# Gated cross-attention and gated MLP on one core: V and A of the decay-weighted output product as pairs of f16 parts in place of fp32r

## The reference, cut to what matters

```
xh, kh   = layernorm(x), context                     # 4 heads of 128 columns
Q,K,V    = xh @ Wh, kh @ Wh, kh @ Wh                 # per head
masked   = (Q @ K^T / sqrt(128)) * decay             # [b, h, s, t]
A        = maximum(abs(masked.sum(axis=0)), 1.0)     # summed over the 64 tiles
O        = A @ V                                     # per head, one A for all tiles
Y        = (O - mean) / sqrt(var + 0.001) * gamma + beta
x        = x + tanh(g0) * (relu(xh @ wg) * Y @ wo)
x        = x + tanh(g1) * (silu(ln(x) @ gate^T * gs) * (ln(x) @ up^T * us)) @ down^T * ds
```

## Time and profile before

| | |
|---|---|
| time, median of 3 | 1442.77 us |
| profiled execution, span | 1447.4 us, granted clock 0.998 |
| TensorE matmul busy | 1420.4 us, 98% |
| VectorE, ScalarE, GpSimd busy | 1043.3, 726.3, 735.3 us |
| attention loop | to about 323 us |
| first `o(0)` | 328.65 us |

### The profile page before, as it was taken

The page is one execution under the profiler, slowest core; times in us unless marked ns, Lnnn a source line. Parts: engine busy times, 40 slices in busy tenths (PEclk is TensorE's granted clock), DMA queues, the critical chain, the costliest instruction groups (busy, mean ns, idle before and its releaser), DMA issues.

```text
span 1447.4 us, 20320 instructions
## 1 busy us (share of the span) xinstructions
PE 1420.4 (98%) x7097; PEld 728.3 (50%) x7135; DVE 1043.3 (72%) x1562; ACT 726.3 (50%) x1145; POOL 735.3 (51%) x734
## 2 busy tenths in 40 slices
PE   8999999999999999999999999999999999999998
PEld 4666666665445544455444444444444444444443
DVE  7788998878477676766776677564867768768762
ACT  5566565554555635455463545534344444443442
POOL 5656769863564445444553554434137237137235
PEclk9999999999999999999999999999999999999999
DMA  8999898973878796987888897886383473572432
GB/s 275 344 336 306 292 317 318 343 251 130 276 204 263 227 276 206 260 276 210 248 274 237 264 243 222 247 252 164 112 228 115 124 224 122 139 218 98 139 109 89
DMA packets 372920, 324.96 MB, mean 225 GB/s; under 512 B 259280, under 2 KB 285264, under 8 KB 372816
## 3 DMA queue, kind: packets, MB, share of 16 engines
q1 hardware_dynamic: 355248, 291.63, 66.2%
q10 hardware_dynamic: 17568, 31.99, 6.2%
HBM read 209.14 MB, written 114.43 MB: 224 GB/s over the span
## 4 chain that ended last, share of the span: by engine, by line
PE 74%; DVE 10%; DMA 6%; SPq 3%; issue 3%; ACT 2%; POOL 2%; ACTq 0%; DVEq 0%; POOLq 0%
PE ps L2067 24%; PE po L2067 8%; PE pyb L1930 7%; PE ps L2074 7%; PE ptb L2074 5%; PE pyb L2074 5%; PE ps L1988 5%; PE po L1930 3%; PE pyb L2058 3%; PE ptb L2058 3%; DMA wy_scratch<-misc 2%; SPq L510 2%; DVE reg L1129 1%; PE ptb L2062 1%; PE pyb L2062 1%
## 5 line engine op out<-in xcount | busy, mean ns | idle before, releaser
L2067 PE MATMUL ps<-x2t,gate 128*128 128x512 f16 x704 | 166.6, 379 | 1.2 <-DVE tmp L1436 1.1
L1930 PE MATMUL pyb<-xnt,wgs 128*128 128x512 f16 x708 | 166.3, 380 | 1.4 <-DVE wgs L1153 1.3
L2067 PE MATMUL ps<-op,wbuf 128*128 128x512 f16 x704 | 166.3, 379 | 0.5 <-issue 0.5
L2067 PE MATMUL ps<-x2t,up 128*128 128x512 f16 x704 | 166.3, 379 | 0.0
L1800 POOL TENSOR_TENSOR p5b<-p5b,p1b 128x512 f32<-128x512 f32 x44 | 55.7, 1265 | 209.1 <-ACT p5b L860 209.1
L1816 POOL TENSOR_TENSOR hid<-tmp,hid 128x512 f16<-128x512 f32 x88 | 104.6, 1190 | 105.9 <-ACT hid L836 105.9
L2074 PE MATMUL ps<-down_first,hid 128*128 128x512 bf16 x683 | 152.4, 379 | 2.1 <-POOL hid L1816 0.8
L1811 POOL TENSOR_TENSOR hsp<-hall,hsp 128x640 f16<-128x640 f32 (+2 forms) x72 | 123.6, 1731 | 37.1 <-ACT hsp L887 37.1
L2067 PE MATMUL po<-op,wbuf 128*128 128x512 f16 x528 | 129.0, 379 | 0.6 <-DVE u2b L1383 0.6
L1436 DVE SCALAR_TENSOR_TENSOR tmp<-ps,colsb,tmp 128x512 f32<-128x512 f32 x88 | 65.4, 744 | 68.2 <-PE ps L2067 62.3
L1988 PE MATMUL ps<-reg 128*128 128x256 f32 x768 | 109.7, 294 | 4.3 <-DVE reg L1129 3.8
(11 more groups left out here) (218 smaller groups left out, 2764.2 us busy)
## 6 DMA issues: line engine op xcount, KB each, us to landing
wbuf<-ws_scratch SPq DMA_DIRECT2D x44, 896.0 KB, 5.0
xr<-in_x SPq DMA_DIRECT2D x62, 512.0 KB, 6.3
raw<-in_ctx_t SPq DMA_DIRECT2D x32, 512.0 KB, 5.6
v_scratch<-tmp ACTq DMA_DIRECT2D x64, 256.0 KB, 6.0
raw<-v_scratch SPq DMA_DIRECT2D x32, 512.0 KB, 6.6
x_scratch<-xr SPq DMA_DIRECT2D x32, 512.0 KB, 4.8
xr<-x_scratch SPq DMA_DIRECT2D x32, 512.0 KB, 5.9
raw<-w_scratch SPq DMA_DIRECT2D x31, 512.0 KB, 6.0
```

What stands on the lines that cost most here:

```text
L1930: last = e.matmul(dst, lhs[a], rhs[b], start=(k == 0 and i == 0), stop=(k == n - 1 and i == 2))
L2067: last = e.matmul(dst, upper(wt), act[i], start=start, stop=stop and exact, skip_group_check=True)
```

## The change

V and A become pairs of f16 parts. f16 has a small range, so each is first multiplied by one number for the whole tensor.

- *V.* ScalarE squares the whole context with an accumulated sum (`ct_square`, two 128x1024 passes per group, written where `ct_hi` writes afterwards; `ct_hi` waits for it). VectorE adds the 32 sums (`ac`), TensorE adds them over partitions (`ct_bound`), VectorE multiplies by a factor from Wh (`am`), GpSimd makes `vk` of it (power -1/2). `v_hi` is an ACTIVATE with scale `vk`, `v_lo` a SCALAR_TENSOR_TENSOR.
- *A.* VectorE takes the row maximum, TensorE turns it (`a_bound`), VectorE reduces it, makes a power of two of it (`ak`) and writes the two parts. The 0.001 of the normalisation becomes a value `eg` from both factors.
- *Order.* `v_hi(0)` comes behind two V evictions and waits for `vk`. GpSimd waits for `am` in front of `weights_residue(6)`. The loads of group 1's context wait for the squares of group 0. Two more quarters of W tile `LATE + 2` run before `o(0)`, and the later quarters move up by one or two places. Two semaphores are merged into others.

```diff
-        a_sb = [placed(f"a{i}", [128, 512], f32r) for i in range(2)]
+        a_parts = [over(f"a_part{i}", f"a{i}", 0, [128, 4, 128], f16) for i in range(2)]
-        vs_later = [part(52 + 4 * i, 512, b=2) for i in range(2)]
+        vs_later = [over(f"vs_later{i}", "reg", 52 + 4 * i, [128, 2, 512], f16) for i in range(2)]
@@ SP: ct_load
                 if g == 1:
+                    p.wait_ge("mass", 7)
@@ ScalarE
+            def ct_square(g, hp):
+                p.wait_ge(f"ct{hp}", 16 * (g + 1))
+                if g >= 2:
+                    p.wait_ge("v", 4 * g - 4)
+                e.activation(ct[1 if g == 0 else g % 2][0][:, 2 * hp:2 * hp + 2, :], raw[:, 2 * hp:2 * hp + 2, :], ACT.Square, scale=2.0 ** -15,
+                             accum_out=csq[:, 2 * g + hp:2 * g + hp + 1]).then_inc(s["mass"])
 ct_hi:
+                p.wait_ge("mass", 5 + 2 * g + h // 2 + 1)
 v_hi:
-                e.copy(vs_of(q)[0], raw[:, 0:2, :]).then_inc(s["vhi"])
+                p.wait_ge("cc", 2)
+                e.activation(vs_of(q)[0][:, :, :], raw[:, 0:2, :], ACT.Identity, scale=vk).then_inc(s["vhi"])
 order, group 0:
             w_store(0)
+            ct_square(0, 0)
+            ct_square(0, 1)
             w_out(1)
...
             w_out(2)
+            ct_square(1, 0)
             ct_hi(1, 0)
...
             v_out(2)
+            ct_square(1, 1)
             ct_hi(1, 2)
 order, groups from 1:
-                else:
-                    v_hi(0)
...
                 v_store(4 * g)
                 if not more:
+                    v_hi(0)
                     w_out(LATE - 1)
...
                 v_store(4 * g + 1)
+                ct_square(g + 1, 0)
                 ct_hi(g + 1, 0)
...
                 v_out(4 * g + 2)
+                ct_square(g + 1, 1)
                 w_out(4 * g + (1 if g < NG - 2 else 0))
@@ VectorE, last group
+                    p.wait_ge("mass", 5 + 2 * NG)
+                    e.tensor_reduce(ac, csq[:, :], AX.X, ALU.add).then_inc(s["cs"])
                 v_acc(4 * g)
+                    p.wait_ge("bound", 3)
+                    e.tensor_scalar(am, ptb[:, 1, 0:1], fk, 1e-30, ALU.mult, ALU.add).then_inc(s["cs"])
@@ VectorE, A
-            e.tensor_scalar(a_sb[0][:, :], xr[:, 7, :], 1.0, None, ALU.max).then_inc(s["ahi"])
-            e.scalar_tensor_tensor(a_sb[1][:, :], xr[:, 7, :], 1.0, f(a_sb[0][:, :]), ALU.max, ALU.subtract).then_inc(s["alo"])
+            p.wait_ge("cc", 2)
+            e.tensor_reduce(am, xr[:, 7, :], AX.X, ALU.max).then_inc(s["ad"])
+            e.tensor_scalar(xr[:, 7, :], xr[:, 7, :], 1.0, None, ALU.max).then_inc(s["ad"])
+            p.wait_ge("bound", 4)
+            e.tensor_reduce(ak[:, 0:1], ptb[:, 1, :], AX.X, ALU.max).then_inc(s["ahi"])
+            e.tensor_scalar(ak[:, 1:2], ak[:, 0:1], 1.0, 2.0 ** -14, ALU.max, ALU.mult).then_inc(s["ahi"])
+            e.tensor_single_scalar(ak[:, 2:3].bitcast(u32), ak[:, 1:2].bitcast(u32), 0x7F800000, ALU.bitwise_and).then_inc(s["ahi"])
+            e.reciprocal(ak[:, 3:4], ak[:, 2:3]).then_inc(s["ahi"])
+            e.tensor_scalar(a_parts[0][:, :, :], wide, ak[:, 3:4], None, ALU.mult).then_inc(s["ahi"])
+            e.scalar_tensor_tensor(a_parts[1][:, :, :], wide, ak[:, 3:4], a_parts[0][:, :, :], ALU.mult, ALU.subtract).then_inc(s["alo"])
@@ GpSimd
+            p.wait_ge("cs", 3)
+            e.tensor_scalar(vk, am, 2.0 ** 30, 1e-30, ALU.mult, ALU.add).then_inc(s["cc"])
+            e.tensor_tensor(vk, vk, nhalf[:, 0:1], ALU.pow).then_inc(s["cc"])
             weights_residue(6)
@@ TensorE
                 v(4 * g + 1, 1)
                 if not more:
+                    ct_bound()
...
-            w(LATE + 2, (0,))
+            a_bound()
+            w(LATE + 2, (0, 1, 2))
             o(0)
...
-            w(LATE + 2, (1, 2, 3))
+            w(LATE + 2, (3,))
+            w(LATE + 3, (0, 1))
             y_t(0)
-            w(LATE + 3, (0, 1))
+            w(LATE + 3, (2,))
             o(1)
-            w(LATE + 3, (2,))
+            w(LATE + 3, (3,))
             y_t(1)
-            w(LATE + 3, (3,))
+            w(LATE + 4, (0,))
             wo_mm(0, (0, 1))
-            w(LATE + 4, (0,))
             y_t(2)
```

More of the change, by code:

```diff
@@ L14 @@
 SEMAPHORES = (
-    ["xt0", "xt1", "xt2", "whr", "whr2", "wgr0", "wgr1", "wgr2", "wgr3", "cols", "rows", "dec", "wor", "dld", "outb", "lowld", "vld"]
+    ["xt0", "xt1", "xt2", "whr", "whr2", "wgr0", "wgr1", "wgr2", "wgr3", "cols", "dec", "wor", "dld", "outb", "lowld", "vld"]
     + [f"xl{i}" for i in range(4)]
@@ L26 @@
     + ["st", "mv", "xn", "tbxe", "tbwe", "tb2e", "scaledlo", "whlo", "ctlf", "zlo", "acc", "and", "xlo", "lowm"]
-    + ["ad", "ahi", "alo", "flag", "vlo", "wolo", "nm", "nr", "aff", "wm", "wylo", "wyb", "x2b", "x1", "st2", "mv2", "nm2", "xn2", "ds", "h", "hlo"]
-    + ["mass", "bound", "lim"]
+    + ["ad", "ahi", "alo", "flag", "vlo", "wolo", "nm", "nr", "aff", "wm", "wylo", "wyb", "x2b", "x1", "st2", "mv2", "nm2", "xn2", "h", "hlo"]
+    + ["mass", "bound", "lim", "cs", "cc"]
     + ["oe", "of", "gs", "top", "topd", "all", "inv", "dpk", "dmv"])
@@ L148, in gated_layer @@
         down = over("down", "xreg", 0, [128, NI, 512])
-        a_sb = [placed(f"a{i}", [128, 512], f32r) for i in range(2)]
+        for i in range(2):
+            placed(f"a{i}", [128, 512])
         xbuf = placed("xbuf", [128, 2, 512])
-        a_parts = [a[:, :].rearrange("p (h n) -> p h n", h=4) for a in a_sb]
+        a_parts = [over(f"a_part{i}", f"a{i}", 0, [128, 4, 128], f16) for i in range(2)]
         reg = placed("reg", [128, 84 * 256], f32r)
@@ L173, in gated_layer @@
         down_first = over("down_first", "reg", 33, [128, NI, 512], bf16)
-        vs_later = [part(52 + 4 * i, 512, b=2) for i in range(2)]
+        vs_later = [over(f"vs_later{i}", "reg", 52 + 4 * i, [128, 2, 512], f16) for i in range(2)]
         x2t = [over(f"x2t{i}", "reg", 68 + 8 * i, [128, 4, 512], f16) for i in range(2)]
         wos = [[over(f"wos{i}{k}", "reg", 4 + 8 * i + k, [128, 512], f16)[:, :] for k in range(4)] for i in range(2)]
-        vs_first = [part(36 + 4 * i, 512, b=2) for i in range(2)]
+        vs_first = [over(f"vs_first{i}", "reg", 36 + 4 * i, [128, 2, 512], f16) for i in range(2)]
         wyt_first = [over(f"wyt_first{i}", "reg", 32 + 2 * i, [128, 4, 128], f16) for i in range(2)]
@@ L213, in gated_layer @@
         yb = tmp[:, 3, :]
+        csq = sb("csq", [128, 2 * NG])
+        scales = sb("scales", [128, 16])
+        fk, am, ac, vk, ak, eg = [scales[:, a:b] for a, b in ((0, 1), (1, 2), (2, 3), (3, 4), (4, 8), (8, 10))]
         sums = [over(f"sums{i}", "wyt0", 12 * i, [128, 6, 4, 128]) for i in range(2)]
@@ L550, in _ @@
             e.dma_start(colsb[:, :], cols).then_inc(s["cols"], 16)
-            e.dma_start(ds[:, :], rows).then_inc(s["rows"], 16)
+            e.dma_start(ds[:, :], rows).then_inc(s["cols"], 16)
             x_load(6)
@@ L899, in silu @@
                 p.wait_ge("gm", m + 1)
-                p.wait_ge("gs", 1)
+                p.wait_ge("gs", 2)
                 if m >= 3:
@@ L1139, in limit_g @@
                 power_above(0, ptb[:, 0, 0:1].bitcast(u32), 0)
+                e.tensor_scalar(fk, ptb[:, 0, 0:1], 2.0 ** -16, 1e-30, ALU.mult, ALU.add).then_inc(s["cs"])
             def limit_wg(step):
@@ L1432, in hidden @@
                 m, n = 11 * g + j, 15 * g + j
-                p.wait_ge("gs", 2)
+                p.wait_ge("gs", 3)
                 p.wait_ge("si", m + 1)
@@ L1440, in finish @@
                 p.wait_ge("dn", t + 1)
-                p.wait_ge("ds", 1)
+                p.wait_ge("gs", 1)
                 p.wait_ge(*yb_read[0])
@@ L1507, in _ @@
                     stats(n + 4)
+                if not more:
+                    p.wait_ge("mass", 5 + 2 * NG)
+                    e.tensor_reduce(ac, csq[:, :], AX.X, ALU.add).then_inc(s["cs"])
                 v_acc(4 * g)
                 if not more:
+                    p.wait_ge("bound", 3)
+                    e.tensor_scalar(am, ptb[:, 1, 0:1], fk, 1e-30, ALU.mult, ALU.add).then_inc(s["cs"])
                     low_sums(3, 2)
@@ L1604, in _ @@
             v_lo(3)
-            p.wait_ge("rows", 16)
+            p.wait_ge("cols", 32)
             p.wait_ge("tg", 1)
             p.wait_ge("inv", 1)
-            e.tensor_scalar(ds[:, :], ds[:, :], tg[:, 1:2], inv[:, 3:4], ALU.mult, ALU.mult).then_inc(s["ds"])
+            e.tensor_scalar(ds[:, :], ds[:, :], tg[:, 1:2], inv[:, 3:4], ALU.mult, ALU.mult).then_inc(s["gs"])
             e.tensor_scalar(colsb[:, 0:NI], colsb[:, 0:NI], 1.0 / UP, None, ALU.mult).then_inc(s["gs"])
@@ L1724, in y_rstd @@
                 p.wait_ge("mv", B + t + 1)
-                power(rs[:, t % 8:t % 8 + 1], mv[:, t % 8, 1:2], 1e-3, "rs")
+                p.wait_ge("ahi", 7)
+                power(rs[:, t % 8:t % 8 + 1], mv[:, t % 8, 1:2], eg[:, 1:2], "rs")
             def y_rstd_pair(q):
@@ L2010, in w, with ct_bound, a_bound @@
                     last.then_inc(s["w"])
```

(9 more changed lines are left out.)

20 lines of the change are left out of this document (14 added, 6 removed).

## The result

The changed kernel takes 1449.62 us (median of 4 runs, 1448.61 to 1452.81), the kernel before, beside it, 1442.62. The ratio is 1.0055, 95% interval 1.0041 to 1.0069: slower by 7.0 us. Forecast were 1445.9 us, +3.1, so the sign came true and the size did not. The time lies 0.6 us above the range.

What follows compares the result with a forecast made beforehand. TensorE, busy 98% of the span, was taken as the bound, with ScalarE at 50%. Start 2.1, middle 0.6, last group 1.1, hand-over 2.9 and f16 -3.6 sum to +3.1: 1445.9 us, range 1441.5 to 1449.0 (8 in 10).

Steps and rivals of the forecast that it cites:

- the middle groups: Context groups between first and last: both squares hidden in ScalarE's slack except behind late stores, +0.6 us, bounds 0 and 4.
- The row of group 10: Profile row before `w_out(40)`: a late store left ScalarE only 0.21 us idle, so 0.45 us of the square shows.
- stores are late in most groups and the middle costs 2 to 3 more: Half of rival "Secondary losses"; the other half is a clock drop after a wait near 38 us; 1448.0 us, chance 0.2.
- The start: Group 1's two squares delay `z_hi(4)`, `z_lo(4)` and TensorE's `z(6)`, with nothing behind absorbing it: +2.1 us.
- with a slow load up to 1 us: Group 0's squares hold back SP's loads of group 1's context: priced at 0, up to 1 us if a load is slow.
- The last group: Last context group: the first square delays GpSimd's full row of copies, so `v(60)` starts later, +1.1 us (0.4 to 1.3).
- The hand-over: Attention loop to first output `o(0)`: new chain to `vk` and A starts `o(0)` 3.2 later; less faster `o`, +2.9 us.
- The lock: In the hand-over, `v_lo(0)` waits for GpSimd's weights residue to end; without it 1.0 us less, rival "No lock" chance 0.25.
- The quarters: W tile quarters moved ahead of `o(0)`: from `o(0)` on they give nothing back.
- The signs: Expected: `o` matmuls 0.109 apart, `z(6)` waiting on `z_lo`, gap before last V product, `v_lo(0)` over 2 us, `o(0)` waiting.
- The f16 products: `o` matmuls 0.109 us each against 0.119, 0.12 us per `o`, thirty in or just before gated layers: -3.6 us.
- The base: Profiled span 1447.4 us, 4.6 above the 1442.77 median, mostly put on a 2.77 us TensorE stall at 772 and slowed clock.

## Why the prediction was right or wrong

**The failed step is the middle groups**, "Second square: 1.83 idle and the same 0.54 against 1.05, hidden" and the sum "+0.6 us in all, bounds 0 and 4". The 28 squares there cost 5.5 to 6.8 us in time by the medians. In the traces the stretch from `z_hi(4)` to `z_hi(60)` is some 4 us longer with them (279.6 in the mean of five profiles, 275.7 in that of eight without), and the single V tiles, with the W tile's wait behind them, account for that much: 48.7 to 50.5 us against 45.1 (46.0 with f16 parts alone). The rest of the loss in time isn't located. One thing was wrong for certain, a second probably.

First, the idle time of an ordinary group was read as slack of all groups. The busy share of 50% is one of the whole span; in the loop, from 40 to 316 us, ScalarE was busy for 167 us of 276 before (61%) and 192 after (70%). ScalarE's waits in that stretch show it whole; the kernel before (second profile), then after:
```profile
ACT tmp L743 <- PE pyb L1930: 28.2, 29, 1.8
...
ACT tmp L735 <- DMA v_scratch<-tmp: 9.1, 7, 2.0
```
```profile
ACT tmp L749 <- DMA v_scratch<-tmp: 9.0, 8, 2.0
ACT tmp L757 <- PE pyb L1977: 8.9, 15, 0.8
```
`w_out` waited for TensorE 29 times before, 15 times after. The V evictions lose 9 us to late stores in both, seven or eight times. In five of those groups too little slack was left, and there the square's 1.25 us fell on TensorE: the W tiles behind the evictions of W tiles 5, 33, 41, 49 and 53 waited 0.93, 0.41, 0.45, 0.32 and 0.88 us, all behind a late store and the second square. In the second profile of the changed kernel two of the seven waits, of 0.55 and 0.41 us, were for W tiles 32 and 52, behind the first square: it isn't always hidden either. The row of group 10 had said it, and I multiplied it by too few groups. My rival "stores are late in most groups and the middle costs 2 to 3 more", part of a case with a chance of 0.2, comes closest to what happened, though late stores mattered in five groups and not in most. Its other half, a fall of the clock, did not: from 40 to 316 us the granted clock was 1.00 in the changed kernel as in the one before.

Second, I priced only the instruction next in line, while what stands further behind a square on ScalarE, and GpSimd's copies of the context with it, can come later too. For a cost of this kind speaks that first squares alone cost some 2 us by the medians, and that moving the second ones brought back little, though hardly a W tile waited in either case. The pairs of V tiles may be the place: 47.9 us with first squares alone, 48.4 and 49.0 with the second ones moved, 47.2 in the mean of the eight profiles without squares in the loop. But one of those eight has 48.6. So this second cost is likely and not shown, and which follower would pass it on isn't settled.

**The start** (+2.1; bounds 1.6 and 2.4) had the right place: `z_hi(4)` at 39.1 against 36.5 and 37.6, TensorE waiting on `z_lo` before `z(6)`. "Nothing behind absorbs it" is not shown: with these four squares alone the kernel measures 1.0008 both times. The "with a slow load up to 1 us" that I allowed for belonged to V's stores, which I had not looked at, and not to the load of the context.

**The last group** (+1.1): GpSimd's copies ended at 320.86 and `v(60)` started at 320.91, but from `z_hi(60)` to it went 2.86 us against 2.47: +0.4, the low bound. TensorE was late itself; it had stood 1.12 us for `z_lo` just ahead:
```profile
319.40 1.47 PE L1977 MATMUL po<-xnt,gs 128*128 128x512 f16 x6 [1.12 <-DVE reg L1149]
```

**The hand-over** (+2.9) was priced too high. The stage from `z_hi(60)` to `y_stats(0)` grew by 2.7, and the next one by nothing, but the last group's +0.4 is part of that: forecast for both together were 4.0. From `v(60)` to `o(0)` it is 15.46 us against 12.82, +2.6 where "`o(0)` +3.2" stood. The chain has the forecast links and the wait on the low part of A (0.42 us in front of `o(0)`). The lock was worth 0.85 by the residue's move (1.0 forecast). The quarters gave back nothing, as forecast. So the last group and the hand-over were 1.3 too high together and hid part of what the middle groups lacked: that the total missed its range by only 0.6 was luck in part.

**The signs.** `z(6)` came 2.6 us later and waited for `z_lo`, `v_lo(0)` took over 2 us, `o(0)` waited for the low part of A, and the `o` products stand 0.109 apart: these came true. The gap in front of the last group's V product didn't. None of the signs looked at the middle groups, so they could hold while the sum failed.

**The f16 products** (-3.6): -1.2 us in the quiet stretch from the 23rd to the 45th `silu`, a quarter of that stage; in one place, 8 matmuls of 512 columns and 12 of `o(q)` took 3.03 us against the 3.16 of the earlier trace rows:
```profile
403.41 1.89 PE L2127 MATMUL ps<-x2t,up 128*128 128x512 f16 x8
405.13 1.47 PE L1977 MATMUL po<-vs_later,a_part 128*128 128x256 f16 x12
406.44 0.81 PE L2127 MATMUL ps<-x2t,gate 128*128 128x512 f16 x3
```
That is 0.109 each (1.31 / 12). Nine `o` products lie in the quiet stretch, so each gave 0.13 us where I took 0.12. In time the f16 parts alone gave 2.7 us, with 3.6 inside the interval (0.7 to 4.6). This term held as far as it can be measured.

**The base.** I put the profiled execution's excess on the stall at 772 us. The second profile of before confirms the place in part: it is 6.5 us shorter, 5.1 of them in the stage with the stall, where TensorE stood 0.59 us in place of 2.77 and the granted clock was 1.00 in place of 0.78. Another 2.5 us lie in the attention loop. I also compared a span with a time: a span is about 2 us less than the time of its own execution, so the excess was nearer 6.8 than 4.6. The sum doesn't hang on it, since the differences are added to the median as well.

## What to carry to other kernels

Before work is put into an engine's idle time, count the occurrences in which that idle time is already gone, by the view of waits over the whole loop and not by one or two groups; an engine with 50% idle time over the whole kernel had too little in a third of the loop's groups, where a V store was late. And before an effect of 1 or 2 us is read from a stage of a profile, look at how far that stage moves between profiles of one kernel. A long loop multiplies a small mistake per turn, so its term needs the widest bounds. And where a scale factor costs 32 passes and a chain of ten small steps at a hand-over, price it first against what the cheaper format gives: here 2.7 us gained against 9.7 spent (7.0 and the 2.7).

## What was unexpected of the hardware

- ScalarE's `v_hi` takes 1.147 us with its scale read from a column; as a plain copy it took 1.044 into fp32r and 1.042 into f16 (f16 parts alone). The groups of ScalarE of the changed kernel, then of the one with f16 parts alone:
```profile
L776 ACT ACTIVATE vs_later<-raw,scales 128x1024 f16<-128x1024 f32 x30 | 34.4, 1147 | 4.1 <-DMA raw<-v_scratch 2.9 <-POOL scales L1918 1.1
```
```profile
L762 ACT CAST vs_later<-raw 128x1024 f16<-128x1024 f32 x30 | 31.3, 1042 | 5.2 <-DMA raw<-v_scratch 5.2
```
- The landing of V's stores, of 256 KB each, moves from execution to execution: `z_hi(4)`, behind an eviction that waits for them, came at 36.5 and 37.6 in two executions of the same kernel. Experiments at that point below 1 us need the median of many runs.
- The same wait near 770 us was 0.59 and 2.77 us in two executions of the kernel before. With the 2.77 came a granted clock of 0.78 over the 5 us from 770, while beside waits of 2.53 and 2.59 us at this place in two other profiles (squares at the start only, moved and not) it stayed at 1.00. So the prediction's reading that such a wait brings the clock down holds for one profile of three.
